# A selective-scan layer: where the loop's diagonal matrices and inputs are made

## The chip, the cores and the metric

The kernel runs on one core of a Trainium2 chip, as one launch. The metric is the device time of that launch in microseconds (us), 1975.6 us before the change. The core's engines work side by side, each through its own list of instructions in order: TensorE (PE in the profile; its weight loads are PEld) multiplies matrices, VectorE (DVE) and GpSimd (POOL) do elementwise work, ScalarE (ACT) evaluates functions, and SyncE (SP) issues DMA transfers. They meet only at semaphores: an instruction raises one by finishing, and another engine waits for its value.

## The reference

The reference is a tower of four layers, each with two parts, on 32 images of 36 patches and a class token: 1184 rows of 256 values. The change touches one part, the selective state-space layer (the third layer's first part). Its core is a recurrence over time, for each of 512 channels d and 16 states n:

```python
def _selective_scan(u, delta, A, Bm, Cm, D):
    b, l, d = u.shape
    n = A.shape[1]
    deltaA = jnp.exp(jnp.einsum('bld,dn->bldn', delta, A))
    dBu = delta[..., None] * Bm[:, :, None, :] * u[..., None]

    def step(state, inp):
        dA_t, dBu_t, C_t = inp
        state = dA_t * state + dBu_t
        y_t = jnp.einsum('bdn,bn->bd', state, C_t)
        return (state, y_t)
    ...
    return y + u * D
```

Ahead of it the normed input is projected, passed through a causal convolution with four taps and a SiLU (this gives u), and projected again to B, C and the step size delta, which goes through a softplus. Behind it, y is multiplied by the SiLU of a second projection and projected back to 256 values, and added to h.

## The kernel before

`stage_scan` holds the layer. Channels lie on the 128 partitions in C = 4 blocks, and time (33 sequences of 37, 1221 columns) is cut in NCH = 3 thirds of CH = 407 columns. In the code u is `xc`, the second projection's SiLU is `res`, and `delta`, `xc` and `res` are tiles of [128, 3, 4, 407]. The stage has two blocks, with a barrier of all engines and the arming of the second block's semaphores (`sems`, lines 38 to 49, one small GpSimd instruction for each) between them.

The first block (lines 2219 to 2461) makes `xc`, `res`, `delta`, and the rows B and C. VectorE norms the input, negates `a` (L2438), does the convolution's taps as ScalarE delivers each channel block (L2442), adds the step size's bias (L2451), and ends with the softplus: for each third, a subtraction (L2459) and a maximum with an addition (L2461). ScalarE evaluates the exponentials and logarithms between, and ends the block with nine SiLUs of `res` (L2371), which follow TensorE's projections. SyncE loads the weights first (L2245 to L2250, among them D as `dd`, tile s_db), and at the end writes B and C to DRAM and loads them back, spread over all partitions, as 16 tiles `bc` (s_bcb).

The second block (L2463 on) is the loop. It has 96 steps k: six units (a third and half of the channel blocks) of 16 states n each. A step works on 2 x 407 = 814 columns:

- ScalarE: the decay exp(delta a), two ACTIVATEs (L2519) into PSUM, and zeros at each sequence's start (L2523). It runs at most two steps ahead.
- GpSimd: the input, `du` times B, into one of DB = 4 buffers `dbu` (L2535); for 3 of 8 states also the scan's result times C (L2543).
- VectorE: the scan (L2626, or L2623 where GpSimd takes the multiplication by C), and for the other states the multiplication by C (L2630).
- TensorE: the sum over n in PSUM, by multiplication with the identity (L2580); at the start of each unit it adds u D, by a diagonal matrix of D, `dg` (L2571), of which there are four.

`du` is delta times u, one VectorE instruction of 1628 columns for each third. Between the steps VectorE also evicts a finished unit (L2600) and adds the projected output to h (L2595). Everything is written out by hand in the order in which each engine does it; no scheduler moves anything. Ahead of step 0, VectorE makes `du` of the first third (L2604), the four `dg` (L2607) and `du` of the second third (L2611); `du` of the last third stands behind step 6. Semaphore c_du tells GpSimd which thirds of `du` are there, and c_dg tells TensorE that the matrices are.

Of the kernel before, what the change touches and what calls it, by code (L numbers as in the profile page):

```python
# [15 lines left out]
ALU = mybir.AluOpType  # L16
# [7 lines left out]
P = 128  # L24
# [6 lines left out]
NCH = 3  # L31
# [6 lines left out]
def sems(nc, stack, names):  # L38

    made = {n: nc.alloc_semaphore(n) for n in names.split()}
    for sem in made.values():
        nc.gpsimd.nop().then_inc(sem, 1)
    nc.all_engine_barrier()
    stack.callback(lambda: nc.clear_and_free_semaphores(list(made.values())))
    return made
# [2142 lines left out]
def stage_scan(nc, d, h, xT, ident):  # L2192
# [5 lines left out]
    with ExitStack() as stack:  # L2198
# [9 lines left out]
        dd = sb("s_db", [P, C])  # L2208
        bc = [sb(f"s_bcb{m}", [P, 2, CH]) for m in range(N)]
        w_out = sb("s_w_outb", [P, C, D])  # L2210
        bc_dram = nc.dram_tensor("s_bc", (NCH, N, 2, CH), F32, kind="Internal").ap()

        def load(sp, t, m):
# [5 lines left out]
        with ExitStack() as inner:  # L2219
# [7 lines left out]
            xdbl = sb2("s_xdbl", [R + 2 * N, T])  # L2227
            small = norm_small(sb2, "sn")
            xp = [sb2(f"s_xpb{k}", [P, B + 1, SP]) for k in range(2)]
            e = sb2("s_eb", [P, NCH, C * CH])  # L2230
            one = sb2("s_oneb", [P, NCH, C * CH])
            xn = e[0:TT, :, :].rearrange("p t x -> p (t x)")[:, 0:NT * D].rearrange("p (t x) -> p t x", x=D)
            acc = [one[:, :, :].rearrange("p t x -> p (t x)")[:, k * T:(k + 1) * T].rearrange("p (b j) -> p b j", j=S)
# [195 lines left out]
            @block.vector  # L2429
            def _(dve):  # L2430
                link = chain(dve, sg["v"], -1)
                norm_dve(nc, dve, sg, link, h, xn, small, 1e-5, True)
                for g, (lo, hi) in enumerate(GROUPS):
                    dve.wait_ge(sg["turned"], KC * g + 1)
                    nc.vector.tensor_copy(xT[:, 0, lo * TT:hi * TT], pp[:, KC * g, 0:(hi - lo) * TT]
                                          ).then_inc(sg["xt_dve"], 1)
                dve.wait_ge(sg["a_exp"], 1)
                nc.vector.tensor_scalar(a[:, :, :], a[:, :, :], -1.0, None, ALU.mult)  # L2438
                for c in range(C):
                    dve.wait_ge(sg["tap0"], c + 1)  # L2440
                    for k in range(1, K):
                        ins = nc.vector.scalar_tensor_tensor(acc[c % 2], xp[c % 2][:, :, k:k + S], cw[:, c, k:k + 1],  # L2442
                                                             acc[c % 2], ALU.mult, ALU.add)
                        if k < K - 1:
                            link(ins)
                        else:
                            ins.then_inc(sg["taps"], 1)
                for i in range(BY_DVE):
                    t, c = divmod(i, C)
                    dve.wait_ge(sg["dt_mm"], i + 1)  # L2450
                    nc.vector.tensor_scalar(delta[:, t, c, :], pp[:, X_BANKS[i % 3], 0:CH], b_dt[:, c:c + 1], None,  # L2451
                                            ALU.add).then_inc(sg["pre"], 1)
                for t in range(NCH):
                    dve.wait_ge(sg["one"], t + 1)
                    nc.vector.scalar_tensor_tensor(one[:, t, :], one[:, t, :], -1.0, e[:, t, :], ALU.add, ALU.subtract
                                                   ).then_inc(sg["ef"], 1)
                for t in range(NCH):
                    dve.wait_ge(sg["ln"], t + 1)
                    link(nc.vector.tensor_tensor(e[:, t, :], e[:, t, :], one[:, t, :], ALU.subtract))  # L2459
                    df = delta[:, t, :, :].rearrange("p c x -> p (c x)")  # L2460
                    nc.vector.scalar_tensor_tensor(df, df, 0.0, e[:, t, :], ALU.max, ALU.add)  # L2461

        with ExitStack() as inner:  # L2463
            sb2, ps2 = bufs(nc, inner)
# [8 lines left out]
            pooled = [0]  # L2473
            for _, n in at:
                pooled.append(pooled[-1] + on_pool[n])
            s = sems(nc, inner, "c_du c_dg c_zero c_exp c_da c_dbu c_scan c_vec c_pool c_sum c_ym c_out_mm c_out")
            landed = [sg[f"bc{m}"] for m in range(N)]
            w_landed = sg["w_out"]
            du = sb2("c_dub", [P, NCH, C, CH])
            dbu = [sb2(f"c_dbub{b}", [P, HW]) for b in range(DB)]  # L2480
            st = [sb2(f"c_st{b}", [P, HW]) for b in range(YB)]
            dg = sb2("c_dgb", [P, C, P])
            zero = sb2("c_zerob", [P, HW // S])
            ycol = sb2("c_ycol", [P, C, T])
            da = [ps2(f"c_da{u}", [P, 2 * BANK]) for u in range(2)]
# [40 lines left out]
            @block.gpsimd  # L2526
            def _(pool):
                def inputs(k):
                    u, n = at[k]
                    t, c0 = units[u]  # L2530
                    pool.wait_ge(s["c_du"], t + 2)
                    pool.wait_ge(landed[n], t * 16 + 16)
                    if k >= DB:
                        pool.wait_ge(s["c_vec"], k - DB + 2)
                    nc.gpsimd.tensor_tensor(wide(dbu[k % DB][:, :]), du[:, t, c0:c0 + HC, :],  # L2535
                                            bc[n][:, 0:1, :].broadcast_to([P, HC, CH]), ALU.mult
                                            ).then_inc(s["c_dbu"], 1)

                def outputs(k):
                    n = at[k][1]  # L2540
                    pool.wait_ge(s["c_vec"], k + 2)
                    one = wide(st[k % YB][:, :])
                    nc.gpsimd.tensor_tensor(one, one, bc[n][:, 1:2, :].broadcast_to([P, HC, CH]), ALU.mult  # L2543
                                            ).then_inc(s["c_pool"], 1)

                for k in range(DB - 1):
                    inputs(k)
                for k, (u, n) in enumerate(at):
                    if k + DB - 1 < K2:
                        inputs(k + DB - 1)  # L2550
                    if on_pool[n]:
                        outputs(k)

            @block.tensor
            def _(pe):
                def project(t, n):

                    pe.wait_ge(s["c_ym"], 2 * t + 3)
                    if t:
                        pe.wait_ge(s["c_out"], done[t] + 1)  # L2560
                    for c in range(C):
                        last = nc.tensor.matmul(slot(t, n), ycol[:, c, n * TT:(n + 1) * TT], w_out[:, c, :],
                                                start=(c == 0), stop=(c == C - 1))
                    last.then_inc(s["c_out_mm"], 1)

                pe.wait_ge(s["c_dg"], C + 1)
                for u, (t, c0) in enumerate(units):

                    pe.wait_ge(s["c_ym"], u + 1)
                    for c in range(HC):  # L2570
                        nc.tensor.matmul(pc[:, c, 0:CH], dg[:, c0 + c, :], xc[:, t, c0 + c, :], start=True, stop=False,  # L2571
                                         skip_group_check=True)
                    for n in range(N):
                        k = u * N + n
                        if on_pool[n]:
                            pe.wait_ge(s["c_pool"], pooled[k + 1] + 1)
                        else:
                            pe.wait_ge(s["c_vec"], k + 2)
                        for c in range(HC):
                            last = nc.tensor.matmul(pc[:, c, 0:CH], ident[:, :], st[k % YB][:, c * CH:(c + 1) * CH],  # L2580
                                                    start=False, stop=(n == N - 1), skip_group_check=True)
                        last.then_inc(s["c_sum"], 1)
                        if t and c0 == 0 and 4 <= n < 4 + done[t] - done[t - 1]:
                            if n == 4 and t == 1:
                                pe.wait_ge(w_landed, 16)
                            project(t - 1, done[t - 1] + n - 4)
                for n in range(done[NCH - 1], NT):
                    project(NCH - 1, n)

            @block.vector  # L2590
            def _(dve):
# [5 lines left out]
                def evict(u):  # L2597
# [3 lines left out]
                                            res[:, t, c0:c0 + HC, :], ALU.mult).then_inc(s["c_ym"], 1)  # L2601

                nc.vector.memset(zero[:, :], 0.0).then_inc(s["c_zero"], 1)
                nc.vector.tensor_tensor(du[:, 0, :, :], delta[:, 0, :, :], xc[:, 0, :, :], ALU.mult  # L2604
                                        ).then_inc(s["c_du"], 1)
                for c in range(C):
                    nc.vector.tensor_scalar(dg[:, c, :], ident[:, :], dd[:, c:c + 1], None, ALU.mult  # L2607
                                            ).then_inc(s["c_dg"], 1)

                def moved_in(t):  # L2610
                    nc.vector.tensor_tensor(du[:, t, :, :], delta[:, t, :, :], xc[:, t, :, :], ALU.mult  # L2611
                                            ).then_inc(s["c_du"], 1)

                moved_in(1)
                for k, (u, n) in enumerate(at):
                    t, c0 = units[u]
                    dve.wait_ge(s["c_da"], k + 2)
# [7 lines left out]
                    else:  # L2625
# [4 lines left out]
                        nc.vector.tensor_tensor(wide(st[k % YB][:, :]), wide(da_k),  # L2630
                                                bc[n][:, 1:2, :].broadcast_to([P, HC, CH]), ALU.mult
                                                ).then_inc(s["c_vec"], 1)
                    if k == 6:
                        moved_in(2)
                    if u and n == 2:
                        evict(u - 1)
                    if t and c0 == 0 and 8 <= n < 8 + done[t] - done[t - 1]:
# [1726 lines left out]
```

## Time and profile before

| what | value |
|---|---|
| three timed runs | 1970.58, 1975.6, 1976.54 us, median 1975.6 |
| the profiled execution | 1971.14 us, its span 1969.3 us |
| mean granted TensorE clock | 0.858 of full speed |
| busy over the span | TensorE 74%, VectorE 73%, ScalarE 41%, GpSimd 30% |
| the state-space layer | 632.8 to 977.9 us of the span |
| its first block | 632.8 to 708.4 us |
| its loop's block | 710.2 to 974.7 us |

The shares over the whole span say little of this layer, since each stage has another limit. So the stage is read by itself: the busy time of each engine in its stretches tells which one has no gap, and the timelines of single engines, put side by side, tell what each first instruction waited for. A timeline row gives the start, the duration, the engine, the line, the output and inputs by the program's tile names with their shapes, and in brackets the idle time of that engine just before, with what ended it. A stretch's row gives its length and the busy time of each engine in it.

### The profile page before, as it was taken

To read this page: it belongs to the slowest core of one execution; us is meant where nothing else is said; L and a number is where in the kernel's file an instruction comes from. 1 tells how busy PE (TensorE), PEld (TensorE's weight loads), DVE (VectorE), ACT (ScalarE), POOL (GpSimd) and SP (SyncE) were. 2 spreads that over 40 slices of the span, in tenths; PEclk is the share of its full clock that TensorE was granted. 3 is DMA by queue.
4 is the path that set the end of the run, shared out by engine and by line. 5 is a ranking of instruction groups with operands and counts; after the bars stand their busy time and mean duration, and the time that the engine had idled before them with its cause. 6 is when DMAs were issued, how large, how long until landed. Compare 5 with 4: busy or idle time off the path is not lost. (4 is left out here: it accounts for less than half of the span.)

```text
span 1969.3 us, 23940 instructions
## 1 busy us (share of the span) xinstructions
PE 1465.7 (74%) x8427; PEld 1153.1 (59%) x8427; DVE 1427.8 (73%) x2337; ACT 810.7 (41%) x1552; POOL 593.0 (30%) x400
## 2 busy tenths in 40 slices
PE   3896323479999947767758951897778889779797
PEld 3574102369998423434448951884357789567697
DVE  7586677898665589999755745787976477675666
ACT  5475220465553755555214521762233243333332
POOL 1500002121220049999515224126212141100320
PEclk8997555889999978998868975899889989878899
DMA  4411000111101212240047511002343010320110
GB/s 97 110 28 44 1 0 0 52 50 43 44 1 39 89 52 67 69 129 8 24 153 175 150 57 44 22 17 40 111 122 86 21 45 11 77 31 2 41 33 26
DMA packets 65313, 108.76 MB, mean 55 GB/s; under 512 B 34750, under 2 KB 43549, under 8 KB 63583
## 3 DMA queue, kind: packets, MB, share of 16 engines
q1 hardware_dynamic: 57218, 92.96, 16.1%
q0 software_dynamic: 6416, 9.29, 2.3%
q10 hardware_dynamic: 1562, 5.00, 0.9%
q8 instruction: 67, 1.10, 0.2%
q14 instruction: 50, 0.41, 0.1%
HBM read 83.82 MB, written 18.13 MB: 52 GB/s over the span
## 5 line engine op out<-in xcount | busy, mean ns | idle before, releaser
L2535 POOL TENSOR_TENSOR c_dbub<-c_dub,s_bcb 128x814 f32<-128x814 f32 x96 | 169.4, 1785 | 84.5 <-DVE c_dub L2604 72.8
L2580 PE MATMUL c_pc<-c_st,ident 128*128 128x407 f32 x384 | 157.8, 560 | 48.4 <-POOL c_st L2543 41.7
L2519 ACT ACTIVATE c_da<-s_deltab,s_ab 128x407 f32<-128x407 f32 x192 | 108.1, 595 | 117.7 <-DVE c_st L2630 100.1
L2580 PEld LDWEIGHTS c_pc<-c_st,ident 128*128 128x128 f32 x384 | 77.4, 209 | 126.1 <-POOL c_st L2543 57.0
L2626 DVE TENSOR_TENSOR_SCAN c_da<-c_da,c_dbub 128x814 f32<-128x814 f32 x60 | 110.6, 1843 | 0.0
L2045 ACT ACTIVATE e_sg<-e_pu,e_b 128x444 f32<-128x444 f32 (+1 forms) x96 | 56.7, 591 | 80.3 <-PE e_pu L1971 74.8
L2126 DVE TENSOR_TENSOR e_sg<-e_sg,e_gate 128x444 f32<-128x444 f32 (+1 forms) x96 | 54.7, 570 | 48.4 <-ACT e_sg L2045 45.4
L3279 DVE SCALAR_TENSOR_TENSOR dc_acc<-dc_pp,dc_cw,dc_acc 128x1311 f32<-128x1311 f32 x48 | 75.9, 1584 | 17.8 <-ACT dc_acc L3212 16.0
L1933 POOL TENSOR_TENSOR e_wlb<-e_wb,e_whb 128x1024 fp32r<-128x1024 f32 x16 | 42.2, 2659 | 126.4 <-ACT e_whb L2020 126.4
L2814 POOL DMA_INDIRECT me_xe<-m_xs,mt_rowsb x48 | 47.9, 998 | 76.7 <-DVE mt_rowsb L2980 36.0
L2543 POOL TENSOR_TENSOR c_st<-c_st,s_bcb 128x814 f32<-128x814 f32 x36 | 68.6, 1905 | 4.6 <-DVE c_st L2623 4.6
L3475 POOL TENSOR_TENSOR do_msb<-do_msb,d_half 111x8 f32<-111x8 f32 x11 | 27.7, 2519 | 137.0 <-DVE do_msb L3736 137.0
L1969 PE MATMUL e_pu<-e_xhb,e_wlb 128*128 128x444 f32 (+1 forms) x192 | 66.8, 348 | 1.1 <-ACT e_sg L2045 1.1
L2623 DVE TENSOR_TENSOR_SCAN c_st<-c_da,c_dbub 128x814 f32<-128x814 f32 x36 | 66.4, 1843 | 0.0
L1970 PE MATMUL e_pu<-e_xlb,e_whb 128*128 128x444 f32 (+1 forms) x192 | 65.8, 343 | 0.0
L1971 PE MATMUL e_pu<-e_xhb,e_whb 128*128 128x444 f32 (+1 forms) x192 | 65.7, 342 | 0.0
L1992 PE MATMUL e_acc<-e_hl,e_whb 128*128 128x444 f32 (+1 forms) x192 | 65.7, 342 | 0.0
L1993 PE MATMUL e_acc<-e_hh,e_wlb 128*128 128x444 f32 (+1 forms) x192 | 65.6, 342 | 0.0
L1994 PE MATMUL e_acc<-e_hh,e_whb 128*128 128x444 f32 (+1 forms) x192 | 65.6, 342 | 0.0
L2630 DVE TENSOR_TENSOR c_st<-c_da,s_bcb 128x814 f32<-128x814 f32 x60 | 60.4, 1006 | 2.1
L2133 DVE TENSOR_TENSOR e_hl<-e_sg,e_hh 128x444 fp32r<-128x444 f32 (+1 forms) x96 | 54.2, 564 | 1.6
L781 ACT ACTIVATE a_e<-a_m,a_nmx 111x37 f32<-111x37 f32 x176 | 48.5, 313 | 12.8 <-DVE a_nmx L832 12.7
(703 smaller groups left out, 4621.9 us busy)
## 6 DMA issues: line engine op xcount, KB each, us to landing
s_bcb<-s_bc SPq DMA_DIRECT2D x48, 407.0 KB, 4.0
m_wb<-in_m_w SPq DMA_DIRECT2D x16, 768.0 KB, 7.5
e_wb<-in_e_w SPq DMA_DIRECT2D x4, 2048.0 KB, 7.5
m_ys<-me_yb SPq DMA_DIRECT2D x16, 384.0 KB
d_z<-d_first ACTq DMA_DIRECT2D x11, 384.0 KB, 2.7
d_first<-d_z SPq DMA_DIRECT2D x11, 384.0 KB, 3.6
le_wb<-in_l_w_e SPq DMA_DIRECT2D x9, 384.0 KB, 3.1
de_wb<-in_d_w_e SPq DMA_DIRECT2D x8, 384.0 KB, 3.1
```

Of the source, the lines that this page charges most:

```text
L1969: nc.tensor.matmul(dst, w_lo, x_hi, start=(k == 0), stop=False)
L1970: nc.tensor.matmul(dst, w_hi, x_lo, start=False, stop=False)
L1971: last = nc.tensor.matmul(dst, w_hi, x_hi, start=False, stop=(k == KC - 1))
L1992: nc.tensor.matmul(dst, w_hi, h_lo, start=(e == 0 and f == 0), stop=False)
L1993: nc.tensor.matmul(dst, w_lo, h_hi, start=False, stop=False)
L2519: last = nc.scalar.activation(da[k % 2][:, c * CH:(c + 1) * CH], delta[:, t, c0 + c, :], ACT.Exp, scale=a[:, n, c0 + c:c0 + c + 1])
L2535: nc.gpsimd.tensor_tensor(wide(dbu[k % DB][:, :]), du[:, t, c0:c0 + HC, :], bc[n][:, 0:1, :].broadcast_to([P, HC, CH]), ALU.mult).then_inc ...
L2543: nc.gpsimd.tensor_tensor(one, one, bc[n][:, 1:2, :].broadcast_to([P, HC, CH]), ALU.mult).then_inc(s["c_pool"], 1)
L2580: last = nc.tensor.matmul(pc[:, c, 0:CH], ident[:, :], st[k % YB][:, c * CH:(c + 1) * CH], start=False, stop=(n == N - 1), skip_group_chec ...
L2623: nc.vector.tensor_tensor_scan(st[k % YB][:, :], da_k, dbu[k % DB][:, :], 0.0, ALU.mult, ALU.add).then_inc(s["c_vec"], 1)
L2626: nc.vector.tensor_tensor_scan(da_k, da_k, dbu[k % DB][:, :], 0.0, ALU.mult, ALU.add).then_inc(s["c_scan"], 1)
L3279: ins = nc.vector.scalar_tensor_tensor(one, pp[u][:, :, k:k + RUN], cw[:, ORDER[c], k:k + 1], one, ALU.mult, ALU.add)
```

## The change

It moves three pieces of VectorE's work, and two tiles with them.

- The four diagonal matrices are made in the first block, between the negation of `a` and the taps, behind a wait for the small loads. The semaphore c_dg and TensorE's wait for it are gone.
- `du` of the first third is made in the first block, behind the softplus of the first third. The tile `du` now lies over `e`, the softplus's scratch. So the instruction that reads `e` is waited for first. GpSimd no longer waits for c_du in the first third.
- `du` of the second third is made behind step 6 and that of the last third behind step 12.

```diff
+        dg = sb("s_dgb", [P, C, P])
+        du = sb("s_dub", [P, NCH, C, CH])
...
-            e = sb2("s_eb", [P, NCH, C * CH])
+            e = du[:, :, :, :].rearrange("p t c x -> p t (c x)")
...
                 nc.vector.tensor_scalar(a[:, :, :], a[:, :, :], -1.0, None, ALU.mult)
+                dve.wait_ge(sg["in"], 96)
+                for c in range(C):
+                    nc.vector.tensor_scalar(dg[:, c, :], ident[:, :], dd[:, c:c + 1], None, ALU.mult)
...
                     df = delta[:, t, :, :].rearrange("p c x -> p (c x)")
-                    nc.vector.scalar_tensor_tensor(df, df, 0.0, e[:, t, :], ALU.max, ALU.add)
+                    ins = nc.vector.scalar_tensor_tensor(df, df, 0.0, e[:, t, :], ALU.max, ALU.add)
+                    if t == 0:
+                        dve.wait_ge(sg["xc"], C)
+                        link(ins)
+                        nc.vector.tensor_tensor(du[:, t, :, :], delta[:, t, :, :], xc[:, t, :, :], ALU.mult)
...
-                    pool.wait_ge(s["c_du"], t + 2)
+                    if t:
+                        pool.wait_ge(s["c_du"], t + 1)
...
-                pe.wait_ge(s["c_dg"], C + 1)
...
-                nc.vector.tensor_tensor(du[:, 0, :, :], delta[:, 0, :, :], xc[:, 0, :, :], ALU.mult
-                                        ).then_inc(s["c_du"], 1)
-                for c in range(C):
-                    nc.vector.tensor_scalar(dg[:, c, :], ident[:, :], dd[:, c:c + 1], None, ALU.mult
-                                            ).then_inc(s["c_dg"], 1)
...
-                moved_in(1)
...
-                    if k == 6:
-                        moved_in(2)
+                    if k in (6, 12):
+                        moved_in(k // 6)
```

VectorE's list across the blocks' boundary, before; c_dub is `du`, c_dgb the matrices, s_eb the scratch `e`, and the branches mark the boundary:

```order
L2459 TENSOR_TENSOR s_eb<-s_eb,s_oneb 128x1628
L2461 SCALAR_TENSOR_TENSOR s_deltab<-s_deltab,s_eb 128x1628
L2219 UNCONDITIONAL_BRANCH
L2590 UNCONDITIONAL_BRANCH
L2603 MEMSET c_zerob 128x22
L2604 TENSOR_TENSOR c_dub<-s_deltab,s_xcb 128x1628
L2607 TENSOR_SCALAR c_dgb<-ident,s_db 128x128 x4
L2611 TENSOR_TENSOR c_dub<-s_deltab,s_xcb 128x1628
L2626 SCALAR_TENSOR_TENSOR c_da<-c_da,c_dbub 128x814
```

Between the zeros and the first scan (the last row) stand six instructions. The same place now, from the first third's softplus on; s_dub is both `e` and `du`:

```order
L2464 TENSOR_TENSOR s_dub<-s_dub,s_oneb 128x1628
L2466 SCALAR_TENSOR_TENSOR s_deltab<-s_deltab,s_dub 128x1628
L2470 TENSOR_TENSOR s_dub<-s_deltab,s_xcb 128x1628
L2464 TENSOR_TENSOR s_dub<-s_dub,s_oneb 128x1628
L2466 SCALAR_TENSOR_TENSOR s_deltab<-s_deltab,s_dub 128x1628
L2464 TENSOR_TENSOR s_dub<-s_dub,s_oneb 128x1628
L2466 SCALAR_TENSOR_TENSOR s_deltab<-s_deltab,s_dub 128x1628
L2221 UNCONDITIONAL_BRANCH
L2597 UNCONDITIONAL_BRANCH
L2610 MEMSET c_zerob 128x22
L2627 SCALAR_TENSOR_TENSOR c_da<-c_da,c_dbub 128x814
```

The zeros are followed by the first scan at once, and the first third's inputs (L2470) stand ahead of the softplus of the other two. In the first block the matrices stand between the negation and the taps:

```order
L2440 TENSOR_SCALAR s_ab<-s_ab 128x64
L2443 TENSOR_SCALAR s_dgb<-ident,s_db 128x128 x4
L2447 SCALAR_TENSOR_TENSOR s_oneb<-s_xpb,s_cw,s_oneb 128x1221 x12
L2456 TENSOR_SCALAR s_deltab<-s_ppb,s_b_dt 128x407 x8
L2460 SCALAR_TENSOR_TENSOR s_oneb<-s_oneb,s_dub 128x1628 x3
```

Before, the first and the third of these rows stood next to each other. Step 12 and what follows it on VectorE, now:

```order
L2627 SCALAR_TENSOR_TENSOR c_da<-c_da,c_dbub 128x814
L2631 TENSOR_TENSOR c_st<-c_da,s_bcb 128x814
L2613 TENSOR_TENSOR s_dub<-s_deltab,s_xcb 128x1628
L2624 SCALAR_TENSOR_TENSOR c_st<-c_da,c_dbub 128x814
L2627 SCALAR_TENSOR_TENSOR c_da<-c_da,c_dbub 128x814
```

The last third's inputs (L2613) are the row that is new here; behind step 6 the same instruction stood before too, and now makes the second third's.

## Rows read from the trace of the kernel before

**Rows 1.** Groups by line, loop's block: busy us, mean ns | idle before
```profile
L2535 POOL TENSOR_TENSOR c_dbub<-c_dub,s_bcb 128x814 f32<-128x814 f32 x96 | 169.4, 1785 | 84.5 <-DVE c_dub L2604 72.8 <-DVE c_st L2630 11.6
...
L2543 POOL TENSOR_TENSOR c_st<-c_st,s_bcb 128x814 f32<-128x814 f32 x36 | 68.6, 1905 | 4.6 <-DVE c_st L2623 4.6
```

**Rows 2.** Busy time by stretch, the loop's scans and the time ahead of them
```profile
720.77:961.94 241.17, 179.59 (x456) 91.88 (x456) 238.87 (x170) 123.98 (x282) 226.53 (x127) 0.89 0.18 56
710.27:720.77 10.50, 3.08 (x4) 1.18 (x4) 10.50 (x8) 3.77 (x7) 6.93 (x4) 0.52 0.00 1
```

**Rows 3.** The line of the diagonal matrices: duration ns min/median/max, first and last start
```profile
L2607 DVE TENSOR_SCALAR c_dgb<-ident,s_db x4: 282/1798/1811, 712.0 to 715.7; 128x128 f32<-128x128 f32 x4
```

**Rows 4.** VectorE's timeline: start us, duration us, what
```profile
701.24 1.85 DVE L2461 SCALAR_TENSOR_TENSOR s_deltab<-s_deltab,s_eb 128x1628 f32<-128x1628 f32 x1
703.01 1.85 DVE L2459 TENSOR_TENSOR s_eb<-s_eb,s_oneb 128x1628 f32<-128x1628 f32 x1
704.89 1.85 DVE L2461 SCALAR_TENSOR_TENSOR s_deltab<-s_deltab,s_eb 128x1628 f32<-128x1628 f32 x1
710.27 1.85 DVE L2604 TENSOR_TENSOR c_dub<-s_deltab,s_xcb 128x1628 f32<-128x1628 f32 x1 [3.53 <-PEq L47]
...
717.41 3.43 DVE L2611 TENSOR_TENSOR c_dub<-s_deltab,s_xcb 128x1628 f32<-128x1628 f32 x1
720.77 1.85 DVE L2626 TENSOR_TENSOR_SCAN c_da<-c_da,c_dbub 128x814 f32<-128x814 f32 x1
...
723.57 1.85 DVE L2626 TENSOR_TENSOR_SCAN c_da<-c_da,c_dbub 128x814 f32<-128x814 f32 x1
...
738.29 2.75 DVE L2611 TENSOR_TENSOR c_dub<-s_deltab,s_xcb 128x1628 f32<-128x1628 f32 x1
740.97 1.84 DVE L2623 TENSOR_TENSOR_SCAN c_st<-c_da,c_dbub 128x814 f32<-128x814 f32 x1
742.73 1.83 DVE L2626 TENSOR_TENSOR_SCAN c_da<-c_da,c_dbub 128x814 f32<-128x814 f32 x1
```

**Rows 5.** GpSimd's timeline
```profile
712.21 6.93 POOL L2535 TENSOR_TENSOR c_dbub<-c_dub,s_bcb 128x814 f32<-128x814 f32 x4 [72.78 <-DVE c_dub L2604]
...
728.36 1.90 POOL L2543 TENSOR_TENSOR c_st<-c_st,s_bcb 128x814 f32<-128x814 f32 x1
730.22 3.50 POOL L2535 TENSOR_TENSOR c_dbub<-c_dub,s_bcb 128x814 f32<-128x814 f32 x2
...
737.57 5.11 POOL L2535 TENSOR_TENSOR c_dbub<-c_dub,s_bcb 128x814 f32<-128x814 f32 x2
```

**Rows 6.** ScalarE's timeline
```profile
710.20 1.28 ACT L2519 ACT_TABLE_LOAD   x1 [1.84 <-PEq L47]
711.50 1.13 ACT L2519 ACTIVATE c_da<-s_deltab,s_ab 128x407 f32<-128x407 f32 x2
712.66 0.19 ACT L2523 ACTIVATE c_da<-c_zerob 128x22 f32<-128x22 f32 x1
...
723.69 1.13 ACT L2519 ACTIVATE c_da<-s_deltab,s_ab 128x407 f32<-128x407 f32 x2 [9.57 <-DVE c_st L2630]
```

**Rows 7.** First block: VectorE's taps, and the stretch 641 to 642 us
```profile
647.99 9.00 DVE L2442 SCALAR_TENSOR_TENSOR s_oneb<-s_xpb,s_cw,s_oneb 128x1221 f32<-128x1221 f32 x6 [5.50 <-ACT s_oneb L2358]
...
641.00:642.00 1.00, 1.00 (x9) 0.72 (x8) 1.00 (x3) 0.91 (x2) 0.00 (x0) 1.00 0.01 4
```

**Rows 8.** The blocks' boundary: duration ns min/median/max, first and last start
```profile
L2219 DVEq DRAIN  x1: 1871/1871/1871, 704.9 to 704.9; - x1
L2219 ACTq DRAIN  x1: 539/539/539, 707.9 to 707.9; - x1
...
L46 POOLq EVENT_SEMAPHORE  x13: 17/17/17, 708.6 to 709.8; - x13
```

**Rows 9.** Stretch 695 to 700 us; last two columns DMA's share and GB/s
```profile
695.00:700.00 5.00, 0.00 (x0) 0.00 (x0) 4.27 (x3) 4.97 (x5) 0.00 (x0) 0.70 0.09 35
```

**Rows 10.** VectorE's first instruction behind the loop's block
```profile
977.99 0.43 DVE L146 BATCH_NORM_STATS2 mn_stats<-h 111x6 f32<-111x256 f32 x1 [3.32 <-PEq L47]
```

More of the change, by code:

```diff
@@ L2475, in stage_scan @@
                 pooled.append(pooled[-1] + on_pool[n])
-            s = sems(nc, inner, "c_du c_dg c_zero c_exp c_da c_dbu c_scan c_vec c_pool c_sum c_ym c_out_mm c_out")
+            s = sems(nc, inner, "c_du c_zero c_exp c_da c_dbu c_scan c_vec c_pool c_sum c_ym c_out_mm c_out")
             landed = [sg[f"bc{m}"] for m in range(N)]
             w_landed = sg["w_out"]
-            du = sb2("c_dub", [P, NCH, C, CH])
             dbu = [sb2(f"c_dbub{b}", [P, HW]) for b in range(DB)]
             st = [sb2(f"c_st{b}", [P, HW]) for b in range(YB)]
-            dg = sb2("c_dgb", [P, C, P])
             zero = sb2("c_zerob", [P, HW // S])
```

## The prediction

> **What bounds the kernel now.** I first looked for the stretch that the change touches: the block ahead of the loop (632.8 to 708.4 us) and the loop's block (710.2 to 974.7 us). The groups of instructions by line of the loop's block [rows 1] show GpSimd with 96 products of 1.79 us and 36 multiplications of 1.91 us. The busy time by stretch [rows 2] shows who is the bound: from the first scan, at 720.77, to the end of the last, at 961.94, VectorE is busy for 238.9 of 241.2 us (the rest is issue gaps), GpSimd for 226.5, ScalarE for 124.0. So the loop is as long as VectorE's list, with GpSimd 6% behind it. The second row of that group is the target: the 10.5 us ahead of the first scan. VectorE is busy there too, but with its own preparation.
>
> The timelines of the engines say what this preparation waits for. VectorE [rows 4] makes the inputs of the first third at 710.27, then the four diagonal matrices, then the inputs of the second third from 717.41 to 720.84, and has its first scan at 720.77. One matrix takes 0.28 us at the least, yet the median is 1.80 [rows 3], and the inputs take 3.43 us at 717.41 against 1.85 at 710.27 [rows 4]. GpSimd runs its first four products in that time [rows 5], and each of these VectorE instructions ends about when a product has ended: the two engines exclude each other in such instructions. ScalarE [rows 6] has loaded its table by 711.48 and has the first decay ready at 712.66 + 0.19 = 712.85; after the second it has nothing to do for 9.6 us. GpSimd has its first product at 712.21 + 1.76 = 713.97, held up by the inputs.
>
> **The change part by part.** (a) The four diagonal matrices go behind the sign change in the block ahead. VectorE then waits 5.5 us for ScalarE's first tap, until 647.99 [rows 7]. The matrices take at most 4 x 0.28 = 1.1 us there, as GpSimd is idle. The new wait for the small loads finds them landed: DMA moves 4 GB/s from 641 to 642 us [rows 7]. Behind it stand the convolution taps, which start at 647.99 as before. Cost nothing; without the cover 1.1 us. TensorE no longer waits for them, and can do the four D matmuls at once; it has slack there either way.
>
> (b) The first third's inputs stand behind the first third's step size, at 699.36, ahead of the second third. Unlinked instructions of this size follow each other after 1.77 us (701.24 to 703.01), linked ones after 1.88 (703.01 to 704.89) [rows 4]. The change links one, since the inputs read what it writes and overwrite what it reads, and adds one: 1.88 us. ScalarE has all logarithms done by then, so only VectorE's own end moves, from 704.89 + 1.85 = 706.74 to 708.62. What held the block's end was ScalarE: its drain ends at 707.9 + 0.54 = 708.4, VectorE's at 704.9 + 1.87 = 706.8 [rows 8]. So 1.7 of the 1.88 us are hidden and 0.2 are not. One semaphore fewer is armed: 13 take from 708.6 to 709.8, 0.1 each. The loop's block starts 0.1 us later. The other end is the full 1.88, if the gap from VectorE's end counts (below).
>
> (c) First scan. It needs the first decay and the first product. ScalarE's chain is not touched (its table load starts at 710.20, before the zeros that its wait is for can be written): 712.85 + 0.1 = 712.95. GpSimd no longer waits for VectorE: its rows B and C landed long ago (DMA 35 GB/s between 695 and 700 us, nothing later [rows 9]), so it starts at about 710.35 and has the first product at 712.1. The scan starts at 712.98 instead of 720.77, 7.8 us earlier. What is late next is ScalarE's table load; from then on ScalarE follows VectorE as before.
>
> (d) Inputs within the loop: of the second third behind step 6, of the last behind step 12. In before, step 6 has one: 738.29 to 740.97, 2.68 us, of which 1.78 are work and 0.9 a wait for the product of 737.57 [rows 4, 5]. Bounds for each of the two now: 1.78 (GpSimd idle) and 1.78 + 1.76 = 3.5 (a product just begun). Where they fall: VectorE asks 738.29 - 720.77 = 17.5 us after the first scan, at 730.5. GpSimd by then has done nine products and two multiplications, at pitches of (6.93 - 1.76)/3 = 1.72 and 730.22 - 728.36 = 1.86 [rows 5]: 19.2 us from 710.35, so its tenth product runs from 729.6 to 731.3, and VectorE waits 0.8. That is 2.6 us. The second comes 2 x 1.76 + 4 x 2.80 = 14.7 us later [rows 4], at 747.8. Continued in the same way, with GpSimd held until 733.1 and then waiting for its buffers, its product 15 ends at 747.8 and the next may only start when step 12 is through: VectorE goes first, 1.8 us. Together 4.4 where before had 2.7: 1.7 us more, bounds 0.9 and 4.3.
>
> (e) GpSimd's products: its lead over VectorE was four at the first scan, and is now half of one. In the same stepping product 3 is there at 717.2 and wanted at 720.2, product 6 at 724.2 for 727.6: the lead grows to the four that its buffers allow, so I cost this at nothing. The inputs of later thirds are written at 733 and 750 us, and product 32 is due about 785. Loads of later rows are issued earlier in step. The tail behind the last scan (GpSimd's product with C, TensorE's sum and projections, the adds) is untouched.
>
> Sum: -7.8 (the later start of 0.1 is in it) + 1.7 = -6.1 us. On the profiled execution, 1971.1 us (span 1969.3), that gives 1965.0; on the median of the three runs, 1975.6, it gives 1969.5. The four times lie in two pairs, near 1971 and near 1976, for no reason that the profile shows, so I name the middle of the two results, 1967.5. A measurement can tell about 0.3%, 5.9 us, from no change, and the forecast lies on that line.
>
> The first scan leans on ScalarE's table load, 1.28 us with the first exponential 0.02 us behind it [rows 6].
> The Trainium skill, "ScalarE: Activation LUTs", section "What ACT_TABLE_LOAD costs", gives every switch another ~1380 ns of drain, some 2.66 us in all; by it the first decay would be ready 1.4 us later and the saving would be 4.7 us. This case's row has no such gap.
>
> **Rivals.** R1, the block's end follows VectorE. Where the loop ends, VectorE's next work comes 3.3 us after its last [rows 10]; here it is 710.27 - 706.74 = 3.5. If that distance is VectorE's and not ScalarE's, all of (b) shows: start +1.88 - 0.1 = 1.8 later, saving 6.1 - 1.7 = 4.4 us, 1971.2 against the median. Against it: VectorE's drain is over at 706.8, 1.6 us before ScalarE's. Chance 0.10.
>
> R2, both inserted inputs meet a fresh product: 7.0 us where I have 4.4, saving 3.5, 1972.1 against the median. For it: at 717.41 that happened (3.43 us). Against: at step 12 GpSimd should be waiting for a buffer. Chance 0.08.
>
> R3, ScalarE's first decay comes later than in before. Its table load lay under 10 us of cover; up to one more load's length, 1.3 us, could appear now that the first scan waits for it. Saving 6.1 - 1.3 = 4.8, 1970.8. For it: the term is exposed for the first time. Against: the load's row [rows 6]. Chance 0.04. The page named above has such a gap.
>
> R4, slower: GpSimd becomes the bound. It is held off by neither inputs nor matrices now, but it has lost its lead, and two waits of 1.78 us for VectorE fall into the first 16 steps. Its chain is 96 x 1.72 + 36 x 1.86 + 3.6 = 235.7 us from 710.35, ending at 946, while VectorE's last scan would end near 955.9; 10 us are free over 132 instructions, so it decides from 0.075 us more each, and the gain is lost at (962.0 - 946)/132 = 0.12 us more, products at 1.9 instead of 1.785. With products at 2.0 us it ends 28 us later, at 974, 12 us behind before's 962: 1987.6. For it: the shares are close (226.5 against 238.9). Against: the same instructions ran at the same pace beside the same scans. Chance 0.06.
>
> **How the numbers follow.** The forecast has 0.72, R1 0.10, R2 0.08, R3 0.04, R4 0.06. Of the forecast's part some two thirds come out over 5.9 us, since a measurement scatters by 2 us and both ends of (d) are open: 0.47, and 0.03 from R1 to R3. Faster by over 0.3%: 0.50, within 0.3%: 0.44, slower: 0.06. The largest saving from the bounds is 7.8 - 0.9 = 6.9 us, the smallest short of R4, with R1 and R2 together, 7.8 - 1.7 - 4.3 = 1.8; as that needs both, I stop at 2.5. From 1970.6 (the lowest run) less 6.9 to the highest, 1976.5, less 2.5: 1963.5 to 1974.
>
> **What would show it.** After the change the first scan starts 2.7 us behind the block's start, set by ScalarE; GpSimd's first product starts with the block; the matrices take 0.3 us each near 642.5, where that gap opens; the block's start moves by 0.1 us (R1: 1.8); the inputs at steps 6 and 12 take 2.6 and 1.8 us; VectorE has no idle time of note before the last scan (R4: waits for products). The forecast is wrong if the first scan still starts over 5 us behind the block's start, or if the distance from the first scan to the last, 241.2 us, grows by over 4 us.

## The result, and the profile after

The change made the kernel faster by 0.2%: 1970.02 us median of 20 runs against 1973.96 of 20 before, ratio 0.998 with a 95% interval of 0.9972 to 0.9988, so 2.4 to 5.5 us. That is in the stated direction, but 3.9 us are less than the 6.1 of the forecast, and below the 0.3% that I had set as a line; the prediction gave 0.44 to an outcome within it. The time is also inside the stated range, 1963.5 to 1974, which says little: the 1973.96 of the kernel before would have been inside it too. The profiled execution's span is 1964.9 us against 1969.3; 1.1 of these 4.4 us lie ahead of the layer (it starts at 631.81 instead of 632.89 us), which no edit touches. So the profiles are compared below by distances within the layer.

VectorE's timeline of the changed kernel at the matrices, the first third's inputs and the first steps:

```profile
641.33 0.87 DVE L2443 TENSOR_SCALAR s_dgb<-ident,s_db 128x128 f32<-128x128 f32 x4
646.92 9.00 DVE L2447 SCALAR_TENSOR_TENSOR s_oneb<-s_xpb,s_cw,s_oneb 128x1221 f32<-128x1221 f32 x6 [4.72 <-ACT s_oneb L2360]
...
698.47 1.85 DVE L2470 TENSOR_TENSOR s_dub<-s_deltab,s_xcb 128x1628 f32<-128x1628 f32 x1
...
709.46 0.08 DVE L2610 MEMSET c_zerob<- 128x22 f32 x1 [1.83 <-PEq L47]
712.06 1.86 DVE L2627 TENSOR_TENSOR_SCAN c_da<-c_da,c_dbub 128x814 f32<-128x814 f32 x1 [2.53 <-ACT c_da L2530]
...
729.60 2.74 DVE L2613 TENSOR_TENSOR s_dub<-s_deltab,s_xcb 128x1628 f32<-128x1628 f32 x1
732.26 1.84 DVE L2624 TENSOR_TENSOR_SCAN c_st<-c_da,c_dbub 128x814 f32<-128x814 f32 x1
...
746.98 1.84 DVE L2613 TENSOR_TENSOR s_dub<-s_deltab,s_xcb 128x1628 f32<-128x1628 f32 x1
748.74 1.84 DVE L2624 TENSOR_TENSOR_SCAN c_st<-c_da,c_dbub 128x814 f32<-128x814 f32 x1
```

The first scan starts 2.60 us behind the zeros, held by ScalarE (L2530), where it was 10.5 us (720.77 - 710.27) [rows 4]. The matrices take 0.87 us in a gap that still has 4.7 us left. The two insertions cost 2.66 and 1.76 us (start to next start). All as forecast. The boundary, to be held against [rows 8]:

```profile
L2221 DVEq DRAIN  x1: 1871/1871/1871, 705.8 to 705.8; - x1
L2221 ACTq DRAIN  x1: 539/539/539, 706.8 to 706.8; - x1
...
L46 POOLq EVENT_SEMAPHORE  x12: 17/17/17, 707.9 to 709.0; - x12
```

VectorE's drain now ends last, at 707.7 against 707.3. From the layer's first instruction to the zeros it is 77.65 us, 77.39 before: 0.26 more.

The busy time by stretch, from the first scan to the end of the last, and from the zeros to the first scan (compare [rows 2]):

```profile
712.06:958.95 246.89, 182.15 (x457) 92.47 (x456) 240.84 (x170) 125.13 (x285) 232.30 (x130) 0.88 0.18 54
709.46:712.06 2.60, 2.60 (x4) 1.05 (x4) 0.08 (x1) 2.56 (x5) 2.60 (x2) 0.51 0.01 3
```

Here is what the forecast did not have: 246.89 us instead of 241.17, 5.7 more where the inputs account for 1.7. VectorE's busy time grew by only 2.0. The rest is idle time, in three rows of its timeline:

```profile
818.98 0.42 DVE L2602 TENSOR_TENSOR h<-h,c_po 111x256 f32<-111x256 f32 x1 [1.43 <-PE c_po L2570]
...
900.64 0.42 DVE L2602 TENSOR_TENSOR h<-h,c_po 111x256 f32<-111x256 f32 x1 [1.68 <-PE c_po L2570]
...
906.83 0.42 DVE L2602 TENSOR_TENSOR h<-h,c_po 111x256 f32<-111x256 f32 x1 [0.87 <-PE c_po L2570]
```

VectorE adds projected output to h behind steps 8 to 10 of unit 2 and 8 to 11 of unit 4 (units and their steps are counted from 0), and now waits 3.98 us in all for TensorE's projections. In before it was one wait of 0.23, in unit 2:

```profile
824.73 0.42 DVE L2595 TENSOR_TENSOR h<-h,c_po 111x256 f32<-111x256 f32 x1 [0.23 <-PE c_po L2562]
```

TensorE's timeline at unit 2, changed kernel:

```profile
802.89 3.08 PE L2578 MATMUL c_pc<-s_xcb,s_dgb 128*128 128x407 f32 x4 [2.84 <-DVE c_ycol L2607]
805.76 8.36 PE L2587 MATMUL c_pc<-c_st,ident 128*128 128x407 f32 x20
813.96 1.89 PE L2570 MATMUL c_po<-s_w_outb,c_ycol 128*111 128x256 f32 x8
```

and the same place in before:

```profile
809.83 3.08 PE L2571 MATMUL c_pc<-s_xcb,c_dgb 128*128 128x407 f32 x4 [3.63 <-DVE c_ycol L2600]
812.71 7.16 PE L2580 MATMUL c_pc<-c_st,ident 128*128 128x407 f32 x20
819.71 1.89 PE L2562 MATMUL c_po<-s_w_outb,c_ycol 128*111 128x256 f32 x8
```

TensorE starts a unit late: it waits for the eviction, which lets it begin 8.39 us behind the unit's first scan in both. It then has the two matmuls with the diagonal matrices and the sums of five steps to catch up on before the first projection (the x20 row, called the 20 sums from here on: each matmul leaves two records). They take 7.16 us where the mean granted clock of that stretch, between its levels of 1.2 and 2.4 GHz, is 0.98 and 8.36 where it is 0.84. The 1.2 us between them are the wait of 1.43 less the 0.23 of before. The two matmuls ahead of them took 3.08 us at 0.50 of full clock in both.

### The profile page after: what moved, and what is told of

It is laid out like the page before. It is cut to its first block and busy times, and to the rows that moved or that the text cites. A ratio compares the mean times of both kernels' runs of the same rounds, so it can differ in the third digit from the quotient of the medians.

```text
span 1964.9 us, 23935 instructions
## 1 busy us (share of the span) xinstructions
PE 1464.5 (75%) x8427; PEld 1150.0 (59%) x8427; DVE 1421.3 (72%) x2337; ACT 810.8 (41%) x1552; POOL 595.0 (30%) x400
## 5 line engine op out<-in xcount | busy, mean ns | idle before, releaser
L2543 POOL TENSOR_TENSOR c_dbub<-s_dub,s_bcb 128x814 f32<-128x814 f32 x96 | 171.0, 1804 | 80.7 <-POOLq L47 71.0
```

## The experiments

Two theories on the missing part. T: TensorE's clock at the start of units 2 and 4 puts the projections behind VectorE's adds. U: these waits are chance in one execution and not what the time lacks. The kernels with e ran on one chip, those with f and g on a second; each ratio is to before on the same chip. The table has VectorE's distances in each profile, in us: zeros to first scan, first scan to end of last scan, and of that the waits for projections between the scans.

| kernel | zeros to scan | scans | waits |
|---|---|---|---|
| before | 10.49 | 241.17 | 0.23 |
| before, second profile | 10.49 | 242.60 | 1.45 |
| changed | 2.60 | 246.89 | 3.98 |
| changed, second | 2.60 | 245.57 | 2.66 |
| changed, third | 2.61 | 245.56 | 2.65 |
| changed, adds later (two profiles) | 2.60 | 242.62 | 0 |
| changed, warm units | 2.60 | 242.62 | 0 |
| matrices only | 5.35 | 244.50 | 2.80 |
| inputs only | 6.87 | 245.66 | 2.76 |
| before, adds later | 10.49 | 240.87 | 0 |
| adds later, inputs first | 3.35 | 242.62 | 0 |
| adds later, inputs behind 12 and 24 | 2.60 | 241.99 | 0 |

**e1, e2 and f4: both kernels again.** No edit. e1 is before:

> The kernel before, unchanged, for a second profile. Theory T: the saving forecast at the first scan is there, and 3.8 us of it are given back since VectorE's adds of units 2 and 4 now wait for TensorE's projections (1.43 + 1.68 + 0.87 us in the trace after, 0.23 before), because the start of these units falls into stretches in which TensorE is granted 1.2 GHz for longer. T expects these mid-loop waits near 0.2 us again, and the distance from the first scan to the start of the last scan's end near 241.2 us. Rival U: the waits are chance from execution to execution; then they may be anywhere from 0 to 4 us here too. The start of the layer (632.9 us in the first trace of before, 631.8 in that of after) should scatter by about 1 us for either.

e2 is the changed kernel, and so is f4, timed on another chip:

> The changed kernel, unchanged, for a second profile. T: mid-loop waits of VectorE for TensorE's projections near 3.8 us again, first scan to end of last scan near 246.9 us. U: anywhere from 0 to 4 us. The first scan starts 2.7 us after the block's start in both.

> The changed kernel once more, timed beside the three others. First scan 2.6 us behind the zeros; first scan to end of last scan 242.6 us plus the waits for projections, which should be 1 to 4 us again. Time 3 to 6 us below before. It says by how much the two partial kernels and the later adds differ from the whole change on one chip.

U has a part: before waits 1.45 us in its second profile where T expected 0.2, and the changed kernel 2.66 and 2.65 where T expected 3.8. But the changed kernel waits longer in each of three profiles than before in either.

The profiles also show what the waits follow. In the seven of them with the adds at step 8 and no added matmuls, the first projection of units 2 and 4 starts 16.71 to 19.71 us behind the unit's first scan, and VectorE's first wait is what exceeds 18.03, in all 14 places to 0.01 us: 19.46 gives 1.43 in unit 2 of the changed kernel, 18.26 gives 0.23 in before, and 16.71, in unit 4 of before, gives none. In that last place the 20 sums took 7.00 us. So the order had 1.3 us to spare with the fastest sums seen, and none with slower ones.

A wait costs a little more than itself. Less its waits the changed kernel takes 242.91 us in each of three profiles, and 242.62 where the adds stand later and nothing waits. f4 came out at 0.9975 of before (0.9959 to 0.999), as in the first comparison. The layer's start lies between 631.3 and 638.3 us over all profiles, which is why spans of single executions say nothing here.

**e3 and g2: adds later.**

```diff
-                    if t and c0 == 0 and 8 <= n < 8 + done[t] - done[t - 1]:
-                        add(done[t - 1] + n - 8)
+                    if t and c0 == 0 and 11 <= n < 11 + done[t] - done[t - 1]:
+                        add(done[t - 1] + n - 11)
```

> The changed kernel with the adds to h of units 2 and 4 three steps later (steps 11 on instead of 8 on), so that TensorE has about 7 us more for the projections that they read; all results stay the same. T: the mid-loop waits go to 0, the loop is 3.8 us shorter than in the trace after, and the time is about 3.5 us below that of the changed kernel, 7 to 8 us below before: 1966. U: the waits go to 0 too, but the mean gain over the changed kernel is half of that or less, 0 to 2 us. If the waits were only a symptom (VectorE would have waited for something else at once), no gain.

The groups by line, the adds' row, changed kernel first, then e3; what is left in e3 lies behind the last scan:

```profile
L2602 DVE TENSOR_TENSOR h<-h,c_po 111x256 f32<-111x256 f32 x11 | 4.4, 414 | 10.5 <-PE c_po L2570 10.5
```

```profile
L2602 DVE TENSOR_TENSOR h<-h,c_po 111x256 f32<-111x256 f32 x11 | 4.3, 410 | 6.5 <-PE c_po L2570 6.5
```

The loop is 4.3 us shorter than in the first profile of the changed kernel: the waits were no symptom. The time was 1965.69 us, ratio to before 0.9946 (0.9931 to 0.996), more than the layer explains. On a second chip:

> The changed kernel with later adds once more, beside g1. On the first chip it came 9.9 us below before in the medians, where the accounts of the layer give 7.89 (first scan) - 0.3 (block start) - 1.7 (inputs in the loop) + 0.2 to 1.5 (before's own waits) = 6.1 to 7.4. The accounts expect 6 to 7.5 here. If some other effect of later adds exists outside the loop, it is 10 again.

0.9965 (0.9946 to 0.9984), 7 us, in line with the layer's account. So I take the first for scatter: the intervals overlap, and e3's seven executions lie between 1962.67 and 1973.72. The second chip also timed the changed kernel (f4, 3 us above g2 in the medians), but not beside it; that later adds gain on the changed kernel rests on the distances in the profiles.

**e4: TensorE kept busy ahead of units 2 and 4.**

```diff
+                    if u in (2, 4):
+                        if u == 4:
+                            pe.wait_ge(s["c_out"], done[1] + 1)
+                        warm(nc, po[:, 0, 0:P], ident, 10)
                     pe.wait_ge(s["c_ym"], u + 1)
```

> The changed kernel with ten more 128x128 matmuls by the identity (their result is overwritten) while TensorE waits for the eviction at the start of units 2 and 4, where it idles for 2.8 and 3.3 us. If the granted clock falls because TensorE idles there, T expects the 20 sums that follow to take 7.0 to 7.2 us instead of 8.4 and 8.6, and VectorE's mid-loop waits to fall from 4.0 us to below 0.5; time about 3.5 us below the changed kernel. If the idle time there is not what lowers the clock (a level granted from further back), the sums stay at 8.4 us and nothing is gained; the extra matmuls may even start the unit 0.5 us late.

TensorE's timeline of e4 at the starts of units 2 and 4 (the ten small matmuls leave 20 records):

```profile
803.59 2.85 PE L100 MATMUL c_po<-ident 128*128 128x128 f32 x20
806.28 1.56 PE L2581 MATMUL c_pc<-s_xcb,s_dgb 128*128 128x407 f32 x4
807.68 7.00 PE L2590 MATMUL c_pc<-c_st,ident 128*128 128x407 f32 x20
...
882.25 2.39 PE L100 MATMUL c_po<-ident 128*128 128x128 f32 x20
886.09 1.64 PE L2581 MATMUL c_pc<-s_xcb,s_dgb 128*128 128x407 f32 x4 [1.44 <-DVE c_ycol L2610]
887.56 7.00 PE L2590 MATMUL c_pc<-c_st,ident 128*128 128x407 f32 x20
```

With its idle time filled, TensorE does the 20 sums in 7.00 us at both places, at a granted clock of 1.00, and the two matmuls ahead of them in 1.56 and 1.64 us. The first projection starts 16.71 us behind the unit's first scan in both units, and the waits are gone without any instruction of VectorE having moved. Ratio 0.9962 (0.9948 to 0.9976). This is one profile, and 7.00 came without the added matmuls too, in unit 4 of before. Together with the 14 places above T holds: it is the clock that makes the projections late.

**f1 and f2: one part each.** f1 makes only the matrices ahead. Against the changed kernel, in the loop's block:

```diff
+                moved_in(0)
+                moved_in(1)
...
-                    if k in (6, 12):
-                        moved_in(k // 6)
+                    if k == 6:
+                        moved_in(2)
```

The first third's inputs are gone from the first block, `e` and `du` are apart again, and GpSimd waits for c_du as in before. f2 takes the matrices out of the first block and puts them back behind the zeros, with TensorE's wait for them:

```diff
                 nc.vector.memset(zero[:, :], 0.0).then_inc(s["c_zero"], 1)
+                for c in range(C):
+                    nc.vector.tensor_scalar(dg[:, c, :], ident[:, :], dd[:, c:c + 1], None, ALU.mult
+                                            ).then_inc(s["c_dg"], 1)
```

> Only the four diagonal matrices move to the block ahead; the inputs of both first thirds stand ahead of the loop as in before. By the accounts of the prediction: the first third's inputs take 1.8 us behind the zeros, the second third's follow before GpSimd has begun, 1.8 us, GpSimd's first product then takes 1.8, so the first scan starts 5.4 us behind the zeros (10.5 in before, 2.6 in the changed kernel), and first scan to end of last scan is 240.9 us without waits for the projections. 5.1 us are saved there, of the 6 that the whole change saves short of these waits. Rival: matrices and inputs share the gain in proportion to their time in the stretch of before (5.4 of 10.5 us), which would be about 4 us. Time near 1970, between 1968 and 1972.

> The inputs move as in the change, the four matrices stay ahead of the first scan. GpSimd now starts its products with the block, so each matrix waits for one product: 4 x 1.8 us, first scan 7.5 us behind the zeros. First scan to end of last scan 242.6 us without waits for projections, as the inputs stand within. The sum of the two is 250.1 us against 251.4 in before: only about 1.3 us saved, less 0.3 for the later start of the block. Rival: moving the inputs by itself saves the 3 to 5 us that they take in before. Time near 1974 to 1975, no difference that can be measured.

Zeros to first scan: 5.35 us (5.4 expected) and 6.87 (7.5). Less the waits, the scans take 241.7 and 242.9, each with the 0.3 that the waits cost beyond themselves. So the matrices alone take 5.1 us off the stretch and need some 0.5 more within the loop, where I expected nothing: the one insertion takes 3.23 us there (start to next start) and 2.68 in before. The inputs alone take 3.6 off and give 1.7 back there. Neither time can be told from before, and f1's gain was expected to show: 0.9992 (0.9975 to 1.0009) and 0.9998 (0.9985 to 1.0011), and both kernels have 2.8 us of waits for projections. VectorE and GpSimd of f2 behind the zeros:

```profile
712.67 1.79 DVE L2610 TENSOR_SCALAR c_dgb<-ident,s_db 128x128 f32<-128x128 f32 x1 [1.92 <-PEq L47]
...
714.38 5.24 DVE L2610 TENSOR_SCALAR c_dgb<-ident,s_db 128x128 f32<-128x128 f32 x3
719.54 1.85 DVE L2628 TENSOR_TENSOR_SCAN c_da<-c_da,c_dbub 128x814 f32<-128x814 f32 x1
```

```profile
712.61 6.92 POOL L2540 TENSOR_TENSOR c_dbub<-s_dub,s_bcb 128x814 f32<-128x814 f32 x4 [71.14 <-POOLq L47]
```

Four matrices end with four products: each waits for one. In the block ahead the same four took 0.87 us.

**f3: adds later, on the kernel before.** The same edit as e3.

> The kernel before with nothing but the adds to h of units 2 and 4 three steps later. If the changed kernel waits more for TensorE's projections than before does (4.0 and 2.7 us in its two traces, 0.2 and 1.45 in before's), this edit gains less here than it did on the changed kernel: 0.2 to 1.5 us, and the loop is 240.9 us. Rival: the later adds gain by something else than those waits, the same 3 us or more on either kernel, with the loop's own length unchanged.

Scans 240.87 us, no waits, as expected; ratio 0.999 (0.9979 to 1.0), which can't be told from no gain. The edit gains 0.3 to 1.7 us of the layer here, against 2.9 to 4.3 on the changed kernel.

**g1 and g3: better places for the inputs.** g1 makes the second third's behind the zeros and the last third's behind step 12; g3 has them behind steps 12 and 24. Both have the later adds.

```diff
+                moved_in(1)
...
-                    if k in (6, 12):
-                        moved_in(k // 6)
+                    if k == 12:
+                        moved_in(2)
```

```diff
-                    if k in (6, 12):
-                        moved_in(k // 6)
+                    if k in (12, 24):
+                        moved_in(k // 12)
```

> The changed kernel with the adds three steps later, and with the second third's inputs made right behind the zeros, in the 2.5 us in which VectorE waits for ScalarE's first decay, instead of behind step 6. GpSimd starts its first product 0.1 us earlier, so VectorE should wait 1.7 us for it and then work 1.8: first scan 3.5 us behind the zeros instead of 2.6. In return only one insertion stands within the loop, behind step 12, where GpSimd waits for a buffer: first scan to end of last scan 240.9 - 2.7 + 1.8 = 240.0 us instead of 242.6. Net 1.7 us less than with later adds alone. Rival: the loop's length does not fall below 240.9, as the place behind step 12 now meets a running product (1 us more), net 0.8. If VectorE goes first, the scan waits for GpSimd's product instead, at the same 3.5 us. Time 1.7 us below the kernel with later adds, which a comparison will hardly tell.

> The changed kernel with later adds and with the two inserted inputs behind steps 12 and 24 instead of 6 and 12. If what an insertion costs depends only on whether GpSimd is within a product, and GpSimd waits for a buffer at both places, each costs 1.8 us: first scan to end of last scan 241.7 instead of 242.6. Rival: a place within the loop costs 2.7 us as a rule, and step 12 was the exception; then 242.6 or 243.5.

g1's first scan came as expected, 3.35 us behind the zeros (3.5 expected), but its scans take 242.62 us instead of 240.0. VectorE's timeline at step 12, and GpSimd's:

```profile
745.98 4.53 DVE L2613 TENSOR_TENSOR s_dub<-s_deltab,s_xcb 128x1628 f32<-128x1628 f32 x1
750.43 1.84 DVE L2625 TENSOR_TENSOR_SCAN c_st<-c_da,c_dbub 128x814 f32<-128x814 f32 x1
```

```profile
745.28 1.80 POOL L2543 TENSOR_TENSOR c_dbub<-s_dub,s_bcb 128x814 f32<-128x814 f32 x1
...
747.01 1.78 POOL L2543 TENSOR_TENSOR c_dbub<-s_dub,s_bcb 128x814 f32<-128x814 f32 x1
```

VectorE asked at 745.98, within one product, and did not come next: GpSimd's next product ran first, and the inputs cost 4.45 us. From the zeros to the last scan's end g1 takes 245.97 us, 0.75 more than later adds alone. g3 takes 244.59, 0.6 less: its insertions cost 2.04 and 1.76 us (1.8 each expected). The medians of g1, g2 and g3 (1977.4, 1976.8, 1977.4, before 1984.4) can't tell them apart; g1's ratio is 0.9973 (0.9955 to 0.9991), g3's 0.996 (0.9939 to 0.998).

## Why the prediction was right in direction and its saving over half too large

(a) Matrices at no cost: right. They take 0.87 us of a gap of some 5.5 us, and f2 shows what they would have cost.

(b) Block's end: right in kind, 0.26 us instead of 0.1. R1 is out, it wanted 1.8: the zeros come 1.8 us behind the later of the two drains in both kernels, while behind VectorE's they come 3.5 us in before and 1.8 now. The length from the layer's start scatters by itself: 77.39, 78.12 (e1) and 77.21 (f3) with the first block of before, 77.65 and 78.73 (e2 and f4) with that of the changed kernel, so 0.1 or 0.3 us is not resolved in it.

(c) First scan 2.7 us behind the zeros: 2.60 in each profile of the changed kernel, and the whole gain of 7.89 us is there. ScalarE's table load is the bound, and showed no cost beyond its row; R3 is out. The Trainium skill, "ScalarE: Activation LUTs", section "What ACT_TABLE_LOAD costs", adds a drain of ~1380 ns to every switch; by that figure the 2.60 would be near 4, as an estimate. No profile here has it: in that of the changed kernel the load takes 1.28 us and the first exponential starts 0.01 us behind it.

(d) Inputs within the loop, 1.7 us: measured 242.62 - 240.87 = 1.75 on the pair without waits (e3, f3). That step 12 cost 1.8 was for the stated reason, but also luck of timing: GpSimd had ended its product at 746.94 and waited for a buffer, and VectorE asked at 746.98. The stated upper bound of one product, 3.5 us, is wrong, as g1's 4.45 shows. R2 did not happen.

(e) GpSimd's supply: right. No scan behind the first waits for a product; R4 is out.

The sum of these terms was right: with later adds, where nothing waits, g2's profile has 7.89 - 0.27 (block's start) - 1.45 (242.62 against 241.17) = 6.2 us less than before's, and 6.1 was forecast. What failed is a step that I passed over in half a sentence, "VectorE has no idle time of note before the last scan". I had taken the 0.23 us wait in before, which I saw in its timeline and left out, for all that TensorE could cost. It was the visible end of a margin that was used up: TensorE catches up on 20 sums before the projections of units 2 and 4, and in each place where they took over 7.1 us VectorE waited. With waits of 0.2 to 1.5 us in before and 2.7 to 4.0 in the changed kernel, the scans' distance grows by 3.0 to 5.7 us, as the profiles are paired; the layer's account is -7.9 + 0.3 and this, so 1.9 to 4.7 us saved. The measured 2.4 to 5.5 fits. The lower end of the stated range is 0.2 us off its own terms (1970.6 - 6.9 = 1963.7), which changes nothing.

Open is why the changed kernel's loop meets the lower clock more often. It does so in the three profiles of the changed kernel and in f1 and f2, but before has two profiles with such adds only, and one of them has 1.45 us. The places of the inputs are not needed for it: f1's VectorE has before's order from the first scan on, and 2.79 us of waits. That the shift of the loop against the clock's rises and falls is the cause was not tested.

## What to carry to other kernels

When the bound engine gets rid of a preparation, look not only at what its first instruction waits for next, but at each place where it already waits a little for another engine: a 0.2 us wait says that this engine has no reserve at the pace it had there. If that engine is TensorE and idles just before, give the consumer a later place in the order: three steps later cost nothing here, and with it the changed kernel is at 0.9946 and 0.9965 of before, with the change alone at 0.998 and 0.9975; the intervals of these overlap in part, the waits in the profiles went from 2.7 to 4.0 us to none. VectorE instructions that exclude GpSimd's products (the matrices, the inputs) belong where GpSimd is idle; beside its products each of them waited between 0 and 2.7 us here.

## What the runs showed of the hardware

A VectorE instruction that is held off by a running GpSimd product need not be next. In g1 it let a second product pass, and waited 2.7 us with products of 1.8. The Trainium skill, "SBUF — State Buffer", section "Who interferes with whom", calls the port pair that these two engines share an exclusive lock; that agrees with the rows of f2 and g1, in which such an instruction ends its wait with a product's end, but it does not say who gets the pair next.

TensorE's granted clock at one place of an unchanged order differs between executions: in f4, e2 and e1, as in the first traces, the 20 sums of unit 2 or 4 take between 7.0 and 8.7 us. In unit 4 of before it is 7.00 in one execution and 8.68 in the other (e1), at 1.00 and 0.81 of full clock. With ten small matmuls in the idle time before them it was 7.00 at both places in e4.
